# Output product of a gated delta-rule layer on 32x32 tiles of TensorE's array instead of 64x64

## The reference

```
x = x + 0.5 * ffn(layernorm(x))
x = x + mixer(layernorm(x))
x = x + 0.5 * ffn(layernorm(x))

ffn:    xr, xk = mix of x and its previous token;  out = sigmoid(xr Wr) * (relu(xk Wk)^2 Wv)
mixer:  q, k, v = silu(causal conv of 4 taps(x W));  q, k normed per head
        16 heads of 16 channels, state S of 16x16 per head and sequence; per token
            S = S * exp(g);  dv = (v - k S) * beta;  S = S + k^T dv;  o = q S
        out = (rmsnorm(o) * norm_w * silu(x Wg)) Wo
```

## Time and profile before

| | us |
|---|---|
| median of 3 runs | 1972.13 |
| lowest and highest run | 1966.24, 1974.1 |
| span of the profiled execution | 1970.6 |

### The profile page before, as it was taken

How to read it: one execution, slowest core, us unless ns; L and a number is a source line. 1 busy time by engine, 2 the same in 40 slices (tenths; PEclk the granted TensorE clock), 3 DMA queues, 4 the chain that set the end, 5 groups by cost and what they waited for, 6 DMA issues and landing times.

```text
span 1970.6 us, 102023 instructions
## 1 busy us (share of the span) xinstructions
PE 1809.7 (92%) x45376; PEld 1515.8 (77%) x45376; DVE 1601.0 (81%) x4326; ACT 1034.9 (53%) x1999; POOL 414.1 (21%) x325
## 2 busy tenths in 40 slices
PE   4689999999999999999999999999999999998886
PEld 3577787887878787878778877878887887787765
DVE  3777898888888888888988888899888889887631
ACT  3644555555555545555555555555555556554422
POOL 0212122222212222221222222122122221221200
PEclk8878999999999999999999999999999999998766
DMA  3000000000000000000000000000000000000000
GB/s 102 1 3 3 14 14 14 4 14 14 14 14 14 9 9 14 14 14 15 14 5 12 14 14 14 14 14 10 7 14 14 14 9 9 9 4 9 8 8 12
DMA packets 21447, 26.26 MB, mean 13 GB/s; under 512 B 2193, under 2 KB 20753, under 8 KB 21009
## 3 DMA queue, kind: packets, MB, share of 16 engines
q1 hardware_dynamic: 21008, 19.73, 3.0%
HBM read 11.33 MB, written 8.39 MB: 10 GB/s over the span
## 4 chain that ended last, share of the span: by engine, by line
PE 76%; DVE 10%; issue 9%; ACT 1%; DVEq 0%; POOL 0%; ACTq 0%; POOLq 0%
PE ps L239 36%; PE ps L221 15%; PE ps L230 9%; PE ps L214 4%; DVE CV L1107 3%; PE ps L411 2%; PE ps L363 2%; PE ps L589 2%; PE ps L579 2%; PE ps L598 2%; PE ps L207 2%; PE ps L381 1%; DVE XR L1384 1%; DVE eg L1364 1%; PE ps L472 1%
## 5 line engine op out<-in xcount | busy, mean ns | idle before, releaser
L1107 DVE SCALAR_TENSOR_TENSOR CV<-ps,cw,CV 128x256 f32<-128x256 f32 x576 | 250.5, 477 | 8.8 <-ACT CV L872 1.9
L239 PEld LDWEIGHTS ps<-QE,S 64*64 64x64 f32 x4096 | 212.4, 140 | 56.7 <-issue 55.2
L239 PE MATMUL ps<-QE,S 64*64 64x16 f32 x4096 | 254.9, 211 | 1.0 <-ACT S L673 1.0
L239 PE MATMUL ps<-WP,V 64*64 64x16 f32 x4096 | 252.5, 210 | 0.0
L239 PEld LDWEIGHTS ps<-WP,V 64*64 64x64 f32 x4096 | 213.4, 140 | 0.0
L239 PE MATMUL ps<-WP,KD 64*64 64x48 f32 x4096 | 144.6, 226 | 28.6 <-issue 26.8
L239 PEld LDWEIGHTS ps<-WP,KD 64*64 64x64 f32 x4096 | 134.4, 141 | 38.7 <-issue 37.4
L1007 POOL TENSOR_TENSOR XK<-XK 128x512 f32<-128x512 f32 x32 | 33.7, 1052 | 608.5 <-ACT XK L846 608.5
L1122 DVE TENSOR_TENSOR prod<-A,TZ 128x30 f32<-128x30 f32 (+7 forms) x480 | 141.4, 295 | 13.2
L239 PEld LDWEIGHTS ps<-SA,M 32*32 32x32 f32 x8192 | 93.2, 109 | 67.3 <-issue 40.5
L221 PE MATMUL ps<-w_r_ffn,XR 128*128 128x256 f32 x512 | 137.6, 416 | 6.7 <-DVE XR L1096 6.7
(11 more groups left out here) (156 smaller groups left out, 4019.8 us busy)
## 6 DMA issues: line engine op xcount, KB each, us to landing
X<-in_x SPq DMA_DIRECT2D x32, 256.0 KB, 2.7
out_x<-X SPq DMA_DIRECT2D x32, 256.0 KB, 2.1
w_r_ffn<-in_wT_r_ffn SPq DMA_DIRECT2D x1, 256.0 KB, 3.3
w_k_ffn<-in_wT_k_ffn SPq DMA_DIRECT2D x1, 256.0 KB, 3.6
w_v_ffn<-in_wT_v_ffn SPq DMA_DIRECT2D x1, 256.0 KB, 4.5
w_k<-in_wT_k SPq DMA_DIRECT2D x1, 256.0 KB, 4.5
w_q<-in_wT_q SPq DMA_DIRECT2D x1, 256.0 KB, 4.8
w_v<-in_wT_v SPq DMA_DIRECT2D x1, 256.0 KB, 5.1
```

What stands on the lines that cost most here:

```text
L239: last = mm(ps[rows, o:o + n], stat[rows, pk].rearrange("p s c -> p (s c)"), mov[rows], **flags)
L1107: last = stt(d4[:, m], src, cw[:, i, m, tap:tap + 1], d4[:, m], ALU.mult, ALU.add)
```

## The change

S4 and V4 (four slots) become S2 and V2 (two slots, half of the columns). `in_slots` then uses the two-slot mask and two activations, and `pairs` issues four products on 32x32 tiles where it issued two on 64x64. The counts in the waits on the two semaphores go with it. Orders, all other products, buffers and banks stay.

```diff
-        K4, KD4, V4, S4 = (sb(n, [P, PACKS, HT, C]) for n in ("K4", "KD4", "V4", "S4"))
+        K4, KD4 = (sb(n, [P, PACKS, HT, C]) for n in ("K4", "KD4"))
+        V2, S2 = (sb(n, [P, PACKS, 2, C]) for n in ("V2", "S2"))
...
-                    pe.wait_ge(s["s_slots"], 4 * g + 4)
-                    pe.wait_ge(s["v_slots"], 4 * g + 4)
+                    pe.wait_ge(s["s_slots"], 2 * g + 2)
+                    pe.wait_ge(s["v_slots"], 2 * g + 2)
...
-                    pairs(o, C, S4, pk, QE[g % 2][:, pk * C:(pk + 1) * C], start=True, stop=False)
-                    last = pairs(o, C, V4, pk, WP[g % 2][:, pk, U:], start=False, stop=True)
+                    pairs(o, C, S2, pk, QE[g % 2][:, pk * C:(pk + 1) * C], start=True, stop=False)
+                    last = pairs(o, C, V2, pk, WP[g % 2][:, pk, U:], start=False, stop=True)
...
-                in_slots(S4, SA[g % 2][:], s["s_slots"])
+                in_slots(S2, SA[g % 2][:], s["s_slots"])
...
-                in_slots(V4, VT[g % NVT][:], s["v_slots"])
+                in_slots(V2, VT[g % NVT][:], s["v_slots"])
...
-                    ve.wait_ge(s["s_slots"], 4 * g - 4)
+                    ve.wait_ge(s["s_slots"], 2 * g - 2)
                 if n == NCH - 1 and g:
-                    ve.wait_ge(s["s_slots"], 4 * g)
+                    ve.wait_ge(s["s_slots"], 2 * g)
...
-                    ve.wait_ge(s["v_slots"], 4 * g - 8)
+                    ve.wait_ge(s["v_slots"], 2 * g - 4)
```

## The result

The kernel after takes 2018.77 us (median of 4 executions, 2003.69 to 2034.05) against 1973.12 us before (4 executions). The ratio is 1.0214, 95% interval 1.017 to 1.0258; it is taken without the execution of 2034.05 us, which lies more than 1.5% above the fastest. The change makes the kernel 2 to 3% slower; 2012 us was forecast. Its profiled execution has a span of 2027.4 us, 57 us over that of before.

What follows compares the result with a forecast made beforehand. TensorE, busy 92% of the span, was taken as the bound. A round: 54.2 - 3.1 + 6.4 stops + 1.5 clock - 0.5 absorbed = 58.5 us against 57.06; 29 rounds add 41 us to 1970.6, giving 2012, range 1937 to 2080.

Steps and rivals of the forecast that it cites:

- Shorter quarters: Each quarter of `o_product` falls from 1.97 to 1.19 us on 32x32 tiles, 3.1 us less TensorE work a round.
- absorb: TensorE's waits for `XN` and `OT` shrink where it falls behind: 0.5 us of 0.9 a round.
- Instructions and packets: 512 more instructions a round from `o_product` to `wo`, 4.8 to 6.83 packets there; about 64 more packets in all.
- Size of the stops: From `o_product` to `wo`, late packets leave TensorE idle 6.4 us a round, bounds 4.2 and 8.1.
- The formula for the stretch: `o_product` to `wo`: 5.83 packet distances of 3.87 us plus one packet's work of 2.66, less 0.6, gives 24.6 us.
- The credit: Work TensorE has in hand when a packet is late, 0.6 us, taken off the time from `o_product` to `wo`.
- Clock: TensorE's lowered clock costs 1.5 us a round after the change, against 1.2 before; bounds 1.2 and 2.4.
- The sum: A round of the full order takes 58.5 us against 57.06, + 1.4 us; over 29 rounds + 41 us.
- Stops do not grow: Rival: TensorE's stops do not follow instruction count, so a round takes 1.7 to 2.3 us less, 1904 to 1924 us; chance 0.13.
- The packet's distance is shorter: Rival: TensorE's packets come 3.5 to 3.65 us apart, stops 4.3 to 5.2 us, 1942 to 1982 us; chance 0.18.
- The clock falls too: Rival: clock stays low through much of the dense stretch, or distances are like 4.15 us; 2065 to 2130 us; chance 0.13.

Runs made afterwards that it cites:

- e3: The kernel after, each output product taking two packs of columns with one stationary (wrong results), as many instructions as before: ratio 0.9804 to before, 1935.44 us.
- e4: The kernel before with `t_product` cut to half its instructions, two packs of columns to a product (wrong results): ratio 0.9808 to before.
- e7: The kernel after with `t_product` cut to half its instructions, two packs of columns to a product (wrong results): ratio 0.9871 to before.
- e5: The kernel before with only quarters 0 and 1 of the output product on 32x32 tiles, four slots kept: ratio 0.994 to before.
- e6: The kernel before with only quarters 2 and 3 of the output product on 32x32 tiles, four slots kept: ratio 1.0183 to before.
- e8: The kernel before with TensorE's `k_squares` moved behind `t_product0` and ScalarE's `k_root` behind `o_root`, same instructions: ratio 1.0021 to before.

## Why the prediction was right

**Shorter quarters.** Right for quarter 0: 1.19 us for 1.97. The round's rest fell by 2.3 us, not by the 3.1 + 0.5 that I had counted. The waits for `XN` stayed (8.7 us in 17 rounds, 9.4 before), and there was little else to absorb. The other part of the gap lies in the dense runs themselves. In the round of after that starts at 611.07 us, quarters 1 to 3 take 1.38, 1.45 and 1.37 us without their stops, and half of `t_product` is longer than in before, with no stop in it and the clock at 1.00. TensorE's timeline, after and before:

```profile
636.92 1.60 PE L240 MATMUL ps<-KP,T 32*32 32x32 f32 x128
```

```profile
1027.17 1.29 PE L239 MATMUL ps<-KP,T 32*32 32x32 f32 x128
```

Why these runs are slower between their stops stays open.

**Instructions and packets.** Right, and the count exact: 64 packets more. That instructions in that stretch cause the stops is shown from both sides, by taking them out (e3, e4, and most cleanly e7) and by adding the same number in two places (e5, e6), and by the distance between stops, never under 254 instructions in after.

**Size of the stops.** Too large: I gave 6.4 us a round, 4.3 was measured, near my lower bound of 4.2. The formula for the stretch held the distance rightly, with a median of 3.84 us in the profile after. Its total also came out: from the first output product to `wo` the kernel after takes 24.4 us on the mean of the 22 rounds, 24.6 was forecast. What was wrong is what fills it. I had 18.2 us of work and 6.4 of stops; it has 20.8 and 3.6 (the other 0.7 us of stops lie elsewhere in the round). The products run at the lower clock for 4.6 us of the stretch, and so some of the time that I had as stops is work that takes longer. The credit, the work in hand when a packet is late, is also too small: in the four rounds whose stretch has the clock at 1.00 throughout it takes 23.4 us, with 4.1 of stops and 19.2 of work. I had calibrated the 0.6 us on a much shorter stretch, and with 1.5 us of stops in it, where of the 1.7 us a round of before only 1.1 lie between the output product and `wo`.

**Clock.** Too small: I charged 1.5 us a round where before had 1.2, + 0.3. The table of the 22 rounds has 0.74 and 2.75, + 2.0. Two errors lie in it. The price from one pair of rounds (1.85 us for about 3.5 us at the lower level, 0.54) is above the 0.37 of 22 rounds; and the time at the lower level grew to 3.6 times, where I had charged a quarter more. I argued that most stops would be near 1.2 us and that part of a lowered clock would be hidden behind the late packets. In the 22 rounds of after each of the 36 falls of the clock comes in or soon after an idle time of 1.06 to 2.03 us, and there are 44 idle times of over 1 us, for 18 in before.

**The sum.** Forecast + 1.4 us a round; measured + 2.4 on the 17 rounds. Stops were over by 2.1 us and clock under by 1.7, and the measured gain was smaller than the forecast one by 0.8 us, by 1.3 with what I had taken as absorbed; the first two nearly cancel. So the direction and its cause were right and the closeness of 2012 to 2019 is partly luck: with the right stops alone (4.3 for 6.4) the sum gives 56.4 us a round, 0.7 under before, and I would have forecast a kernel faster by 1%.

**The rivals.** "Stops do not grow" is out. The Trainium skill ("Runtime: NRT & Kernel Launch", Instruction fetch mechanics) puts 256 instructions to a block of 16 KiB, and 64 packets for 16384 instructions agree; that crossing a block is "mostly hidden" does not hold in this kernel, where it costs 1.7 us a round before and 4.3 after. "The packet's distance is shorter" (3.5 to 3.65 us) is out as the usual case, by the median of 3.84 us, though a quarter of the pairs in the kernel after are 3.59 us apart or less. "The clock falls too" was partly what happened, at a smaller size of stops than I had tied it to.

## What to carry to other kernels

On TensorE count instructions as well as work: in this kernel a stretch of several packets with less than about 3.85 us of work for 256 instructions stops, and the profile shows it as "issue" waits in the middle of a run. One short dense run, such as quarter 0 here, can pass without a stop. Smaller tiles trade work for instructions, so use them where wide products stand between the runs, not all over. A gain in TensorE's work that turns into idle time can be charged twice, since the clock may then fall (e3: 5.0 us idle and 7.6 us at the lower level in a round).

## What the runs showed of the hardware

The instruction packets are 256 to the count (64 packets for 16384 instructions). Two late ones in a row are mostly some 3.84 us apart (after, 3.56 to 5.04); over all traces the pairs reach from 3.30 to 5.50 us. TensorE's granted clock falls to 1.2 GHz with idle times of one to two microseconds even when 88% of the whole span is busy (after, 1.06 to 2.03 us), and it does so with waits for another engine (e3, mostly 2.4 us) as with late instructions. It does not fall each time: in after 8 of 44 idle times of over 1 us have no fall with them, and in e8 it fell with idle times of 0.70 us. What size and spacing of idle times decide it stays open; no run here separates it from the kind of work around.
